# Seven block products in the place of eight in the first layer of a mixture of experts

## What is computed

```
x += sum over e of  weight[token, e] * (gelu(x @ W1[e] + b1[e]) @ W2[e] + b2[e])     W1: 256 x 1024, W2: 1024 x 256
out = (x - mean) / sqrt(var + eps)
```

## Time and profile before

| what | value |
| --- | --- |
| median of 3 runs | 3642.85 us (3634.6 to 5818.66) |
| the profiled execution | 3642.7 us |
| its span | 3640.9 us |
| mean granted clock of TensorE | 0.975 |
| PE busy | 3403.1 us, 93% |
| DVE, ACT, POOL busy | 59%, 53%, 40% |

### The profile page before, as it was taken

How to read it: one execution, slowest core, us unless ns; L and a number is a source line. 1 busy time by engine, 2 the same in 40 slices (tenths; PEclk the granted TensorE clock), 3 DMA queues, 4 the chain that set the end, 5 groups by cost and what they waited for, 6 DMA issues and landing times. The chain is left out here.

```text
span 3640.9 us, 92882 instructions
## 1 busy us (share of the span) xinstructions
PE 3403.1 (93%) x37088; PEld 2355.4 (65%) x37088; DVE 2148.7 (59%) x4708; ACT 1923.6 (53%) x2769; POOL 1460.5 (40%) x1340
## 2 busy tenths in 40 slices
PE   5899999999999999999975887899999999999998
PEld 3667666676766767667653564566666666666666
DVE  4666667666676666767637887444434443444456
ACT  4677676777777677776744665222223222323222
POOL 1343343433334333343326442444444444444443
PEclk8999999999999999999997998999999999999999
DMA  3101111001111011110011121200000000000000
GB/s 119 40 28 34 34 51 41 28 28 40 49 35 37 28 40 46 39 37 28 29 37 60 54 64 57 96 12 12 16 8 24 0 24 0 24 0 12 0 18 29
DMA packets 103874, 123.85 MB, mean 34 GB/s; under 512 B 17664, under 2 KB 94208, under 8 KB 101120
## 3 DMA queue, kind: packets, MB, share of 16 engines
q1 hardware_dynamic: 103520, 118.78, 9.9%
HBM read 50.13 MB, written 8.39 MB: 16 GB/s over the span
## 5 line engine op out<-in xcount | busy, mean ns | idle before, releaser
L2272 POOL TENSOR_TENSOR e_hT<-e_h,e_hT 128x512 f16<-128x512 f32 x512 | 591.8, 1157 | 776.0 <-DVE e_hT L2238 776.0
L981 DVE TENSOR_REDUCE mx<-maxima_pair 128x4 f16<-128x1024 f32 (+1 forms) x384 | 470.2, 1225 | 243.7 <-PE maxima_pair L480 241.2
L2238 DVE CAST e_hT<-e_h 128x512 f16<-128x512 f32 x512 | 301.0, 591 | 455.4 <-ACT e_h L2193 455.4
L75 PE MATMUL bank<-xT,w_half 128*128 128x512 f16 x2304 | 537.3, 384 | 3.9 <-DVE xT L924 3.9
L787 ACT ACTIVATE PR<-scores_pair 128x1024 f32<-128x1024 f32 x384 | 392.5, 1022 | 128.9 <-PE scores_pair L497 120.7
L2193 ACT ACTIVATE e_h<-scores_pair,e_b 128x512 f32<-128x512 f32 x256 | 176.0, 688 | 493.8 <-PE scores_pair L75 442.7
L2193 ACT ACTIVATE e_h<-maxima_pair,e_b 128x512 f32<-128x512 f32 x256 | 176.0, 688 | 457.4 <-PE maxima_pair L75 441.1
L1091 POOL TENSOR_TENSOR hT<-h,hT 128x512 f16<-128x512 f32 x256 | 296.4, 1159 | 265.2 <-ACT hT L774 225.8
L1084 POOL TENSOR_TENSOR QK<-qk,QK 128x512 f16<-128x512 f32 x128 | 148.3, 1159 | 630.5 <-ACT qk L719 435.4
L75 PEld LDWEIGHTS bank<-xT,w_half 128*128 128x128 f16 x2304 | 216.9, 99 | 247.7 <-issue 15.1
L75 PE MATMUL bank<-w_half,hT 128*128 128x256 f16 x3072 | 360.9, 275 | 7.3 <-ACT oT L746 4.6
(11 more groups left out here) (180 smaller groups left out, 6084.9 us busy)
## 6 DMA issues: line engine op xcount, KB each, us to landing
QS<-QK SPq DMA_DIRECT2D x240, 128.0 KB, 2.1
KS<-QK SPq DMA_DIRECT2D x192, 128.0 KB, 2.1
PR<-in_expert_weights SPq DMA_DIRECT2D x16, 1024.0 KB, 5.1
...
```

Source lines behind the costliest of these rows:

```text
L75: last = pe.matmul(out, stat(a, k), mov(b, k), start=(k == 0 and n == 0), stop=(k == tiles - 1 and n == 2))
L981: dve.tensor_reduce(out, src, AX.X, ALU.max, negate=True).then_inc(mx_in.sem, 1)
L2238: dve.tensor_copy(hT[odd][0][:, m, :], h32[:, m % 2, :]).then_inc(h_h.sem, 1)
L2272: pool.tensor_tensor(low, h32[:, m % 2, :], hT[odd][0][:, m, :], ALU.subtract)\
```

## The change

The first layer takes two groups (a pair, 1,024 tokens) at once and treats it as a product of 2 x 2 blocks: on the weights' side features k and halves c of the 1,024 hidden columns, on the inputs' side features k and groups. Seven products of sums of blocks take the place of the eight products of blocks, and four output blocks are put together from them by seven additions.

- **Sums of blocks.** Four of the seven operands on each side are sums. Those of the inputs (`B`) are made once by GpSimd, in expert 0, from a float32 copy of the transposed inputs (`stage`, two groups at a time, 1 MB). Those of the weights (`A`) are made by VectorE for each expert, in place. Then ScalarE and VectorE split all seven into halves, 128x512 at a time: `xB` for the inputs (all four pairs stay in SBUF), `w1` for the weights. `cross` therefore writes the transposed inputs as float32 (`last_full`, `turned`) in the place of the halves; it loads and sums the first operands of expert 0 at its end.
- **Rounds.** The stage is 8 experts x 4 pairs x 4 rounds = 128 rounds, all written out. A round i makes hidden blocks i and i + 4 for both groups: seven products of 3 matmuls x 512 columns each, in the order `P_ORDER` through the four banks `HB`. ScalarE copies the first product to SBUF (`copy`), VectorE does seven additions of a bank and an SBUF tile (`add`), ScalarE does Gelu in SBUF and now also the cast (`gelu`, `high`), GpSimd the low half as before (`low`). `SUM_OF` says which addition frees which bank.
- **Outputs.** Second products of a round are 8 tiles x 2 hidden blocks x 3 terms, 6 matmuls of 256 columns for each tile. They stay in PSUM over the four rounds of a pair, two tiles to a bank, and VectorE adds them to `x` once every four rounds, in the first round of the next pair. Biases come in the other three rounds.
- **Norm.** The last expert norms a pair (8 tiles) at a time: statistics in the second round of the next pair, the rest in its third.

The diff, cut to its core:

```diff
-                sp.wait_ge(s.sem, s.after(n))
-                sp.dma_start(xT_halves[half, :, :, n * GT:(n + 1) * GT], xT[1][half][:, :, :])\
-                  .then_inc(halves_out.sem, 16)
+        def turned(n):
+            sp.wait_ge(xf2.sem, xf2.after(n))
+            sp.dma_start(xT_f32[:, :, n * GT:(n + 1) * GT], xT32[:, :, :]).then_inc(xT_out.sem, 16)
+        def first_pair():
+            sp.wait_ge(xT_out.sem, xT_out.after(1))
+            sp.dma_start(shared["stage"][:, :, :], xT_f32[:, :, 0:2 * GT]).then_inc(shared["first_x"], 16)
...
         def last_high(n, k):
             act.wait_ge(T2_ps.sem, T2_ps.after(n, k + 1))
             if k == 0:
-                act.wait_ge(halves_out.sem, halves_out.after(n - 1))
                 act.wait_ge(R_ps.sem, R_ps.after(n - 1))
             act.activation(xT[1][0][:, k, :], work("T2", n, k)[:, :], ACT.Copy).then_inc(xh2.sem, 1)
+        def last_full(n, k):
+            if k == 0:
+                act.wait_ge(xT_out.sem, xT_out.after(n - 1))
+            act.activation(xT32[:, k, :], work("T2", n, k)[:, :], ACT.Copy).then_inc(xf2.sem, 1)
...
-        def first_expert(i):
+        def first_expert():
             act.wait_ge(O_ps.sem, O_ps.after(NG - 1))
-            act.wait_ge(s_e_raw[i], 16)
-            act.activation(expert_first(shared, i, 0), expert_raw(shared, i), ACT.Copy, scale=WS).then_inc(s_e_hi[i], 1)
+            act.wait_ge(s_e_raw[0], 16)
+            for p in A_ORDER:
+                act.activation(expert_half(shared, 0)[:, p - 1, :], A[p], ACT.Copy, scale=WS).then_inc(s_e_hi, 1)
...
@@ -1657,6 +1670,8 @@
             if has(n - 2):
                 hidden_full(n - 2, 3)
                 hidden_high(n - 2, 3)
+            if n == NG + 1:
+                first_expert()
...
         def last_low(n, k):
-            dve.wait_ge(xh2.sem, xh2.after(n, k + 1))
+            dve.wait_ge(xf2.sem, xf2.after(n, k + 1))
             dve.tensor_tensor(xT[1][1][:, k, :], work("T2", n, k)[:, :], xT[1][0][:, k, :], ALU.subtract)\
...
+        def first_expert_low():
+            for i, p in enumerate(A_ORDER):
+                dve.wait_ge(s_e_hi, i + 1)
+                dve.scalar_tensor_tensor(expert_half(shared, 1)[:, p - 1, :], A[p], WS,
+                                         expert_half(shared, 0)[:, p - 1, :], ALU.mult, ALU.subtract)\
+                   .then_inc(s_e_lo, 1)
+        def first_expert_sums():
+            dve.wait_ge(s_e_raw[0], 16)
+            for i, p in enumerate((7, 5, 6, 3)):
+                if i > 0:
+                    dve.wait_ge(s_e_sum, i)
+                if p in (6, 3):
+                    dve.wait_ge(s_e_lo, {6: 2, 3: 1}[p])
+                first_weight_sum(dve, A, p).then_inc(s_e_sum, 1)
...
+def first_weight_blocks(shared):
+    own = blocks_of(expert_raw(shared, 0).rearrange("p (k n) -> p k n", k=KD))
+    s3 = shared["PR"][0].rearrange("p s n -> p (s n)")[:, KD * F:KD * F + QUARTER]
+    return {1: own[0, 0], 2: own[1, 0], 4: own[1, 1], 5: own[0, 1], 6: own[0, 0], 3: own[1, 0], 7: s3}
+def first_weight_sum(engine, A, p):
+    out, a, b, op = {7: (A[7], A[1], A[5], ALU.subtract), 5: (A[5], A[5], A[4], ALU.add),
+                     6: (A[6], A[5], A[1], ALU.subtract), 3: (A[3], A[2], A[6], ALU.subtract)}[p]
+    return engine.tensor_tensor(out, a, b, op)
...
+    PLACE = ((0, 0), (1, 1), (0, 1), (1, 0))
+    h32 = [sb(f"e_h32_{i}", [P, 4, GT], F32) for i in range(2)]
+    common = sb("e_common", [P, GT], F32)
+    hT = [[sb(f"e_hT{i}_{h}", [P, 2, 2 * GT], F16) for h in range(2)] for i in range(2)]
...
+    P_ORDER = (1, 2, 6, 7, 5, 3, 4)
+    P_AT = {p: i + 1 for i, p in enumerate(P_ORDER)}
+    SUM_OF = {2: 1, 6: 2, 7: 3, 5: 5, 3: 6, 4: 7}
+    BLOCK_SUM = (1, 5, 6, 7)
+    def bank_of(r, p):
...
+        def product(r, p):
+            e, pair, i = place(r)
+            if e == 0 and i == 0:
+                wait(pe, x_lo, pair, X_AT[p])
+            if i == 0 and pair == 0:
+                if e > 0:
+                    wait(pe, w1_lo, e - 1, A_AT[p])
+                elif p in (5, 6, 3, 7):
+                    pe.wait_ge(first_lo.sem, first_lo.upto(0, (5, 6, 3, 7).index(p) + 1))
+            before = r * PRODUCTS + P_AT[p] - 1 - len(HB)
+            of, was = before // PRODUCTS, P_ORDER[before % PRODUCTS]
+            if was == 1:
+                wait(pe, snap, of)
+            else:
+                wait(pe, added, of, SUM_OF[was])
+            for n, (a, b) in enumerate(((0, 0), (0, 1), (1, 0))):
+                last = pe.matmul(bank_of(r, p), w1[e % 2][a][:, p - 1, i * P:(i + 1) * P], xB[b][:, pair, p - 1, :],
+                                 start=n == 0, stop=n == 2)
+            last.then_inc(P_ps.sem, 1)
+        def outputs(r, u):
+            if r < 0:
+                return
+            e, pair, i = place(r)
+            tile = T_ORDER[u]
+            if i == 0:
+                wait(pe, y_x, r // NI - 1, (u | 1) + 1)
+                if u == 0 and pair == 0:
+                    if e > 0:
+                        wait(pe, w2_lo, e - 1)
+                    else:
+                        pe.wait_ge(first_lo.sem, first_lo.upto(0))
+            if u % TT == 0:
+                wait(pe, h_l, r, 3 if u == 0 else 4)
+            for f in range(2):
+                for n, (a, b) in enumerate(((0, 0), (0, 1), (1, 0))):
+                    last = pe.matmul(y_bank(tile), hT[r % 2][a][:, f, tile * P:(tile + 1) * P],
+                                     w2[e % 2][b][:, i + f * NI, :], start=i == f == n == 0 and u % 2 == 0,
+                                     stop=i == NI - 1 and f == 1 and n == 2 and u % 2 == 1)
+            if i == NI - 1 and u % 2 == 1:
+                last.then_inc(Y_ps.sem, 1)
+        for r in range(ROUNDS):
+            product(r, 1)
+            product(r, 2)
+            product(r, 6)
+            outputs(r - 1, 0)
+            product(r, 7)
+            outputs(r - 1, 1)
+            product(r, 5)
+            outputs(r - 1, 2)
+            product(r, 3)
+            outputs(r - 1, 3)
+            product(r, 4)
+            for u in range(4, PT):
+                outputs(r - 1, u)
+        for u in range(PT):
+            outputs(ROUNDS - 1, u)
...
+        def copy(r):
+            wait(act, P_ps, r, P_AT[1])
+            wait(act, added, r - 1, 4)
+            act.activation(common[:, :], bank_of(r, 1), ACT.Copy).then_inc(snap.sem, 1)
+        def gelu(r, j):
+            e, pair, i = place(r)
+            wait(act, added, r, BLOCK_SUM[j])
+            m = i + PLACE[j][0] * NI
+            act.activation(h32[r % 2][:, j, :], h32[r % 2][:, j, :], ACT.Gelu, bias=b1[:, e, m:m + 1], scale=1.0 / WS)\
+               .then_inc(h_f.sem, 1)
+        def high(r, j):
+            f, t = PLACE[j]
+            wait(act, h_f, r, j + 1)
+            act.activation(hT[r % 2][0][:, f, t * GT:(t + 1) * GT], h32[r % 2][:, j, :], ACT.Copy).then_inc(h_h.sem, 1)
+        x_high(0, 1)
+        x_high(0, 2)
+        x_high(0, 5)
+        first_weights_high(5)
+        x_high(0, 3)
+        first_weights_high(6)
+        x_high(0, 6)
+        first_weights_high(3)
+        act.wait_ge(s_b1, 16)
+        for r in range(ROUNDS):
+            e, pair, i = place(r)
+            copy(r)
+            if r == 0:
+                x_high(0, 7)
+                first_weights_high(7)
+                x_high(0, 4)
+            gelu(r, 0)
+            high(r, 0)
+            if e == 0 and pair < NP - 1:
+                for p in ((), (), (1, 2, 5, 3), (6, 7, 4))[i]:
+                    x_high(pair + 1, p)
+            if e < E - 1:
+                for p in {5: (2, 1), 9: (4,), 13: (5, 6), 14: (3, 7)}.get(r % (NP * NI), ()):
+                    weights_high(e + 1, p)
+                for j in {14: (0,), 15: (1, 2, 3)}.get(r % (NP * NI), ()):
+                    second_weights_high(e + 1, j)
+            for j in (1, 2, 3):
+                gelu(r, j)
+                high(r, j)
+            if r == 0:
+                for j in range(4):
+                    second_weights_high(0, j)
...
+            if p in (6, 3):
+                wait(dve, w1_lo, e - 1, A_AT[{6: 1, 3: 2}[p]])
+            first_weight_sum(dve, A, p).then_inc(w_sum.sem, 1)
+        def weights_low(e, p):
+            wait(dve, w1_hi, e - 1, A_AT[p])
+            low(w1[e % 2][1][:, p - 1, :], A[p], w1[e % 2][0][:, p - 1, :], w1_lo)
+        def add(r, n):
+            h = h32[r % 2]
+            out, part, p, made = (None, (h[:, 0, :], common[:, :], 2, 0), (common[:, :], common[:, :], 6, 0),
+                                  (h[:, 3, :], common[:, :], 7, 2), (h[:, 2, :], common[:, :], 5, 2),
+                                  (h[:, 1, :], h[:, 3, :], 5, 3), (h[:, 2, :], h[:, 2, :], 3, 4),
+                                  (h[:, 3, :], h[:, 3, :], 4, 5))[n]
+            if n == 1:
+                wait(dve, snap, r)
+            if n in (1, 5, 4, 3):
+                wait(dve, h_l, r - 2, {1: 1, 5: 2, 4: 3, 3: 4}[n])
```

(91 more changed lines are left out.)

428 lines of the change are left out of this document (219 added, 209 removed).

## The result

The changed kernel takes 3590.45 us (median of four runs, 3585.70 to 3599.90), beside 3638.72 for the kernel before (median of four, one of which took 5818.66 and is not in the ratio). The ratio is **0.987, interval 0.984 to 0.991**: faster by 1.3%, clear of the noise but within 2%. The forecast was 3573, a ratio of 0.981. The profiled execution took 3585.7 us (span 3584.1), 57.0 less than the one the sum was made against, where 69.7 less was forecast.

What follows compares the result with a forecast made beforehand. TensorE's column count was taken to bound the expert stage. From 3642.7 us: - 82.9 - 6.1 + 5 + 1 + 8 + 4.2 + 1.5 = 3573, range 3559 to 3592.

Steps and rivals of the forecast that it cites:

- 1, columns: Expert stage's first products: seven products for eight remove 384 matmuls of 512 columns on TensorE, 82.9 us gained.
- 3, loop turns: Expert stage: written-out rounds remove the two loop turns' idle and slow matmuls, 6.1 us gained, longer code costing nothing.
- Part 4: Start of expert stage: first second product near 20.8 us, 2.5 us at low clock; net +5 us (2 to 10).
- Part 5: Attention stage before the experts: float32 copies on ScalarE have room and the border stays; +1 us (0 to 10).
- Part 6: Expert stage: VectorE steps with two SBUF inputs and GpSimd hold each other, at some rounds; +8 us (0 to 26).
- Part 7: Last expert: three norms delay add 1, +4.2 us (0 to 10); tail after the last products, +1.5 (0 to 4).
- Parts 1 to 3: Expert stage: fewer columns, other engines' work fitting a 9.77 us round with 1.6 us in hand, and no loop turns.
- Rival (c): Steady rounds: the chain add, Gelu, cast, low half does not close in a round; slower than before; chance 0.04.
- Rival (a): Expert stage: two-input VectorE steps and GpSimd do not hold each other, the +8 falls to 0, 3565; chance 0.12.
- (b): Stage before the experts: float32 copies delay the attention chain at every group, 3582; chance 0.06.
- (d): Written-out code is fetched too slowly on some engine, losing the loop-turn gains, 3579; chance 0.04.

Runs made afterwards that it cites:

- eight: Changed kernel with product 4 of every round multiplied twice into its bank, restoring the column count of eight products: 3665.2 us, ratio 1.007.
- bias_mid: Changed kernel with biases moved inside their rounds, one after add 2, one after add 6, only every third after add 7: 3579.4 us, ratio 0.982.
- after_again: The changed kernel run again unedited, for its spread: 3595.6 us, ratio 0.987.
- second_early: Changed kernel with the second weights' high halves cast before the first Gelu in round 0: 3588.0 us, ratio 0.986.
- lows_two: Changed kernel with second weights' high halves early and two of their four low halves moved from round 0 to round 1: 3594.6 us, ratio 0.987.
- all_five: Changed kernel with norm split over two rounds, biases inside rounds, input halves over three, second weights' highs early, two lows moved to round 1: 3569.7 us, ratio 0.980.

## Why the prediction missed

The same terms, by the two profiled executions. The start is 17.1 lost plus 2.15 from the border to the first matmul, less 11.7; the last expert's 16.1 are three norms of 5.2 and 0.4 at the end, where 12.1 us in place of 10.05 follow the last matmul.

| part | forecast | measured |
|---|---|---|
| 1, columns (1,333.2 less 1250.8) | -82.9 | -82.4 |
| 3, loop turns | -6.1 | -6.1 |
| 4, start | +5 | +7.5 |
| 5, stage before | +1 | -0.3 |
| none, the decoder ahead | 0 | -6.2 |
| 6, VectorE beside GpSimd | +8 | +12.3 |
| 7, norm | +4.2 | +15.7 |
| 7, tail | +1.5 | +2.5 |
| sum | -69.7 | -57.0 |

The median of 3590.45 lies near the upper end of the range of 3559 to 3592, but that range was worked out against 3642.7. As ratios it is 0.977 to 0.986, and the measured 0.987 lies above it.

**Parts 1 to 3 were right.** The round is 9.77, no PE idle for issue is left behind the border, and *eight* shows that the columns are the time: put back, they cost 82.8 us of round length. Rival (c) is out: in 900 us of the middle TensorE is busy for 898.48, so the chain closes in a round.

**Part 7 is the step that failed**, in its size. It put the norm "6 us behind biases" and add 1 "about 1.4 after PE wants its bank". The norm did take 5.97. The biases in front of it were priced at 0.48 each, though Part 6 had them held, and took 3.12 in place of 1.4, so that 1.4 became 3.4 (1.7 of the 2.0 us; the other 0.3 is not traced). And behind each wait of 3.4 us matmuls ran in part at the lower clock, 1.85 us more (5.26 less 3.41), which I had charged at the start and at the loop turns but not here. The experiments show both: with six of eight biases in GpSimd's gaps a norm costs 1.7, three of them 5.2, near the forecast 4.2; without biases it costs 1.15 and the window's clock is 1.00. Three norms were thus forecast at 4.2 us and cost 15.7, the largest single miss.

**Part 6 had the right mechanism.** Rival (a), no holding, is refuted: bias_mid shows the holding by place alone (0.47 against 1.34 us in one round). The rule of the Trainium skill (SBUF — State Buffer, "Who interferes with whom"), that one of the two engines is shut out for whole instructions, agrees with these rows (in the row at 3461.48 the second and third bias took 1.43 and 1.37 us, the first, ahead of the subtractions, 0.48) and with the adds' 0.69 us. The Trainium skill says there too that "issue order, not op shape, decides who blocks"; the two outcomes of *after_again* fit that, but its rows do not show which engine was granted first. The places between the experts came to 4.0 (forecast 3.5). Expert 0 came to 8.35 (forecast 4.5), and 13.7 in the second execution: I counted two late rounds a pair, but pairs 1 and 2 also have round 1 or 2 late with the next expert's first weights, and the dearer outcome of the tie with GpSimd was not in the sum. The bound of 26 covered it.

**Part 4** was 2.6 us short at the first second product (23.4 against 20.8); the low clock behind it cost 2.3, forecast 2.5. Of the 2.6, 1.4 is GpSimd's third sum, late behind three VectorE steps in a row; the chain had it at 1.2 without a wait (its six terms add up to 6.3, where the prediction went on with 6.8). All of the 2.6 I have only read, not tried; of the rest the rows show this much: the first two input halves on VectorE took 2.83 us, beside GpSimd's sums. *second_early* and *lows_two* move round 0 by 1.5 and 3.7 us, so the weights' halves do set its end.

**Part 5** was right about the attention stage: from its `c_half` to the last router step it takes 366.0 us, 366.3 before. It is not always so: in the eleven traces with this stage it takes 364.7 to 368.4 in nine, 371.2 in *bias_mid* and 373.2 in *all_five*, which leave it alone; why stays open. The 6.2 us ahead of it belong to a program that the change leaves alone; in *after_again*, whose border is at 2277.58, 1.8 of them are left. That was luck: without it the first execution would be 50.8 us below the old one, not 57.0. Rivals (b) and (d) did not occur.

In short: one interaction, priced in Part 6 and forgotten in Parts 4 and 7, and the lower clock behind the waits of 3.4 us.
